# Scatters of the second-order records moved from the adjacency stage to the propagation layers, through HBM in chunks of 50 columns

## The chip, the cores and the metric

The kernel runs on one core of one Trainium2 chip, as one program. The metric is the time of one execution in microseconds (us); smaller is better. The engines are TensorE (PE, with its weight loads as PEld), VectorE (DVE), ScalarE (ACT), GpSimd (POOL) and SyncE (SP). SP and ACT issue plain DMAs, POOL issues indirect ones (a row of an HBM table per partition, by an index) and, after the change, plain ones too. All of them run on the core's 16 DMA engines.

## The reference, cut to what matters

The input is a graph of 3125 nodes with 48 features each and 100,000 edges (`src`, `dst`, 40 attributes, a type of 8, two weights). Four graph layers follow one another, and after each the result is added to `x` and normalized:

1. an attention network with a gate on each edge and four rounds of attention;
2. a propagation with K = 5 steps, each a sum over the edges with weights from the degrees;
3. a propagation with K = 10 steps, weighted by `edge_weight`;
4. a relation layer.

The last one is what the moved scatters are for:

```python
h1 = relu(einsum('ni,rij->nrj', x, weight1) + bias1)
h2 = einsum('nrj,rjo->nro', h1, weight2)
msg = h2[src, rel_type] * edge_weight1
agg = segment_sum(msg, dst, num_segments=3125)
x = layernorm(x + relu(agg + bias2))
```

## The kernel before, in words

Nodes are cut into 25 blocks of 128 (`NB`). The edges lie in SBUF as 125 partitions by 800 columns (`EP`, `ET`): column t holds 125 edges. Two orders of the edges are made and written to HBM as tables of records:

- `REC`, the first order: a record of 104 numbers for each edge, sorted by pair of source and destination block, in 1488 tiles of 128 edges, four tiles to a group (372 groups).
- `REC2`, the second order: a record of 4 numbers for each edge (weight, two lanes, an index), sorted by destination block, in 816 tiles (204 groups). Only the relation pass reads it, at the very end.

The stages follow one another. Each is a function with a block of its own, and all engines meet at a block's end.

- **`sort_edges`** works out the places. It fills `meta` (6 numbers an edge, 125 x 800 x 6) and at its end `place2` (one index an edge), both kept in SBUF until `adjacency` is done. Its second block runs 25 laps of 4 slots; in each slot POOL waits for semaphores of three kinds of work and then issues 8 scatters into `REC` (L455), one for each column, 800 in all.
- **`tile_tables`** makes small tables.
- **`adjacency`** runs over the 372 groups of the first order. ACT loads a group's records (L763), VectorE builds one-hot matrices (L820, L826, L832), PE transposes them (L791, L792) and multiplies them (L800, L801), ACT copies the transposes (L775) and stores them to `OHT` (L777), VectorE adds the products into `acc` (L846, four to a group), and SP stores each of the four sums to `ADJ` (L737). The order of work on each engine is written out by hand (`in_turns`), with four slots. Beside it, POOL runs a loop of its own: it issues 800 scatters of the second order (L746), one for each column, without a wait between them, and then waits for all of them (L750). Nothing else in the stage needs their result.
- The attention stages follow. From `start_nodes` on, `mem["sums"]` holds 25 x 49 numbers in each partition; attention writes and reads it, the propagation layers don't touch it, and the relation pass writes it again at its end.
- **`propagate`** (L1798) is called twice, with 5 steps and one round for the degrees, and with 10 steps: 16 rounds in all. In a round PE multiplies the features of each of the 25 source blocks with that block's row of the dense `ADJ` (L1874; a row is 1600 KB). Seven of the rows stay in SBUF (`held`, loaded by ACT, L1901). The other 18 pass through three slots: SP waits until PE has used a slot (`s_used`) and loads the next row (L1845). At the end of a round VectorE combines the sums (L1966 and its like), PE transposes them back (L1893), and ACT copies them to the features for the next round (L1908). POOL has nothing to do in it.
- **`relation_nodes`** computes `h2` and stores it.
- **`relation_pass`** runs over the 204 groups of `REC2`: SP loads the records (L2092), POOL gathers four times 128 rows of `h2` (L2104), VectorE makes one-hots and messages (L2135, L2138), and PE adds them up (L1228).

Of the kernel before, what the change touches and what calls it, by code (L numbers as in the profile page):

```python
# [17 lines left out]
I32 = mybir.dt.int32  # L18
# [14 lines left out]
EP = 125  # L33
ET = E // EP
# [8 lines left out]
CW, W, NORM, SL, DL, GIDX = 50, 51, 52, 53, 54, 55  # L43
GATES = 56
RW = GATES + H
META = GATES - CW
# [7 lines left out]
FIRST = 2048  # L54
SW = H + 1
SPB = 10
ROW = 2 * P * NB
HOT = 3
CAP = 60.0
# [648 lines left out]
def adjacency(nc, mem):  # L708
# [3 lines left out]
    with ExitStack() as ctx:  # L712
        room = Room(nc, ctx, "a_")
# [6 lines left out]
        ptr = [room.ps(f"ptr{b}", [P, G, 2, P], BF16) for b in range(2)]  # L720
        sums = [room.ps(f"sums{b}", [P, G, 2 * P]) for b in range(2)]
        s_rec, s_oht, s_out = ([room.sem(f"{name}{b}") for b in range(SLOTS)] for name in ("s_rec", "s_oht", "s_out"))
        s_second = [room.sem(f"s_second{b}") for b in range(4)]
        s_hs, s_wide, s_hot, s_ptr, s_sums, s_turned, s_acc, s_init = (
            room.sem(n) for n in ("s_hs", "s_wide", "s_hot", "s_ptr", "s_sums", "s_turned", "s_acc", "s_init"))

# [14 lines left out]
        with nc.Block() as block:  # L741
            @block.gpsimd
            def _(pool):

                for t in range(ET):
                    nc.gpsimd.indirect_dma_start(  # L746
                        out=mem["REC2"], out_offset=bass.IndirectOffsetOnAxis(ap=mem["place2"][:, t:t + 1], axis=0),
                        in_=mem["meta"][:, t, NORM - CW:META], in_offset=None).then_inc(s_second[t % 4], 16)
                for b in range(4):
                    pool.wait_ge(s_second[b], 16 * ET // 4)  # L750

            @block.sync
            def _(sp):
# [103 lines left out]
def scratch(nc):  # L857

    def dram(name, shape, dt=F32):
        return nc.dram_tensor(name, shape, dt, kind="Internal").ap()  # L860

    mem = {}
    mem["REC"] = dram("REC", [T * P, RW])
    mem["REC_G"] = mem["REC"].rearrange("(g p r) w -> g p (r w)", p=P, r=G)
    mem["REC2"] = dram("REC2", [T2 * P, META - 2])
    mem["REC2_G"] = mem["REC2"].rearrange("(g p r) w -> g p (r w)", p=P, r=G)
    mem["OHT"] = dram("OHT", [NG, P, G * HOT * P], BF16)
    mem["H2"] = dram("H2", [NB * P, RELS * H])
    mem["ADJ"] = dram("ADJ", [(NB + 2) * ROW, P])
    for name, shape, dt in (("ident_bf", [P, P], BF16), ("ident_hf", [P, P], F16), ("ident", [P, P], F32),  # L870
                            ("apart", [P, P], BF16), ("upper", [P, P], F32), ("lower", [P, P], F32),
                            ("iota", [P, P], F32), ("iota_bf", [P, P], BF16), ("cap", [P, G], F32)):
        mem[name] = nc.alloc_sbuf_tensor("m_" + name, shape, dt)
    return mem
# [93 lines left out]
def nodes(ap):  # L968

    return ap.rearrange("p c w -> p (c w)")  # L970
# [824 lines left out]
                norm(nc, dve, ch, sc, out, mem["x"][:])  # L1795


def propagate(nc, mem, half, steps, degrees):  # L1798


    SLOTS = 3
# [9 lines left out]
    with ExitStack() as ctx:  # L1811
# [6 lines left out]
        if degrees:  # L1818
# [4 lines left out]
        s_used, s_f, s_dve, s_deg, s_root, s_x, s_up, s_back, s_sum = (  # L1823
            room.sem(n) for n in ("s_used", "s_f", "s_dve", "s_deg", "s_root", "s_x", "s_up", "s_back", "s_sum"))
        s_tick = room.sem("s_tick")
        acc = room.ps("acc", [P, FOURS, 512])
        back = room.ps("back", [P, 2, 2, 512])
        rows = mem["ADJ"][0:NB * ROW].rearrange("(s p h d) c -> s p h (d c)", s=NB, p=P, h=2)
# [10 lines left out]
        with nc.Block() as block:  # L1839
            @block.sync  # L1840
            def _(sp):
                with sp.Fori(0, rounds) as k:
                    for m, s in enumerate(PASSING):
                        sp.wait_ge(s_used, k * len(PASSING) + m + 1)
                        sp.dma_start(row[:, m % SLOTS], rows[s, :, half]).then_inc(s_row[m % SLOTS], 16)  # L1845

            @block.tensor
            def _(pe):
# [332 lines left out]
def gnn_stack(nc, io, out):  # L2181
    mem = scratch(nc)
# [14 lines left out]
            attention_pass(nc, mem, layer)  # L2197
            update(nc, mem, io, layer)
    residual_norm(nc, mem, mem["x"][:], mem["h"][:], 0)
    propagate(nc, mem, 0, 5, 1)  # L2200
    residual_norm(nc, mem, mem["x"][:], mem["h"][:], 1)
    propagate(nc, mem, 1, 10, 0)
    residual_norm(nc, mem, mem["x"][:], mem["h"][:], 2)
    relation_nodes(nc, mem, io)
    relation_pass(nc, mem)
# [26 lines left out]
```

## Time and profile before

| what | value |
|---|---|
| time of 3 runs, median (lowest to highest) | 11525.92 us (11525.92 to 11526.84) |
| time of the profiled execution | 11507.11 us |
| span of the profiled execution | 11505.3 us |
| PE, DVE, ACT, POOL busy, share of the span | 70%, 55%, 29%, 40% |
| adjacency stage, with POOL's scatters | 1595 to 2787 us |
| adjacency stage, after them | 2790 to 3936 us |
| first and second propagation layer | 8680 to 9242 us, 9259 to 10062 us |

The profile comes from one execution. Its span is the time from the first instruction to the last that the trace shows, and the program's own time is 1.8 us longer. A row of a view groups instructions: the line of the kernel, the engine, the operation, the tile written and those read, the count; then the busy time and the mean duration of one; then the idle time of the engine just before them and what ended it. `issue` means that the engine waited for nothing that the profile shows, `remote` that a semaphore was set from elsewhere. Tile names carry the prefix of their stage: `a_` adjacency, `p_` propagation, `l_` relation pass. The tables `REC` and `REC2` have one name in the rows, `REC`. Stages are told apart by their windows, in us from the start of the span.

### The profile page before, as it was taken

What the parts mean: (1) busy time and instruction counts of PE and PEld (TensorE: products, weight loads), DVE (VectorE), ACT (ScalarE), POOL (GpSimd) and SP (SyncE); (2) the same over time, 40 slices, a digit from 0 to 9 for tenths busy, and PEclk for the clock granted to TensorE, in tenths of its full rate; (3) what the DMA queues carried; (4) which work ended last, traced back from release to release, by engine and by line L of the source; (5) the groups of instructions that cost most, each with busy time, mean ns of one, the idle gap of its engine ahead of it and who ended that gap; (6) DMA issues with size and microseconds to landing.
All of it is one profiled execution on the core that took longest, in us unless ns stands there. A gap on an engine that the chain in (4) does not pass through costs nothing. (4 is left out here: it accounts for less than half of the span.)

```text
span 11505.3 us, 328287 instructions
## 1 busy us (share of the span) xinstructions
PE 8060.2 (70%) x107650; PEld 6419.3 (56%) x107651; DVE 6381.7 (55%) x21371; ACT 3299.7 (29%) x11512; POOL 4649.4 (40%) x6184
## 2 busy tenths in 40 slices
PE   2999943234777588499599769949967889962323
PEld 1777732223555477499489659938963444443323
DVE  6444453335999767688678958868872010011112
ACT  3222211112333233266256536626640000010000
POOL 0777767775000166255145415514530000026665
PEclk9999985555767699799699879969988999955555
DMA  7222223334777699399279649928957889801112
GB/s 293 59 59 59 59 59 79 72 81 120 222 223 222 179 292 311 101 248 248 71 215 248 177 111 248 248 60 226 247 141 294 356 343 372 354 24 18 18 18 18
DMA packets 2228522, 1954.48 MB, mean 170 GB/s; under 512 B 1472897, under 2 KB 1871505, under 8 KB 2189698
## 3 DMA queue, kind: packets, MB, share of 16 engines
q1 hardware_dynamic: 1872642, 1712.86, 48.6%
q10 hardware_dynamic: 252000, 173.83, 4.9%
q0 software_dynamic: 103712, 65.58, 3.8%
q8 instruction: 102, 1.67, 0.1%
q14 instruction: 66, 0.54, 0.0%
HBM read 1478.99 MB, written 470.93 MB: 169 GB/s over the span
## 5 line engine op out<-in xcount | busy, mean ns | idle before, releaser
L1615 POOL TENSOR_TENSOR s_rest<-s_msg 128x196 f32<-128x196 f32 x1488 | 764.3, 514 | 2232.9 <-ACT s_msg L1597 1821.5
L2104 POOL DMA_INDIRECT l_row<-H,l_rec x816 | 786.9, 964 | 2158.9 <-DMA l_rec<-REC 1839.1
L1214 PE MATMUL s_gotd<-m_table_d,s_hot 128*128 x17856 | 1423.5, 205 | 201.1 <-DMA s_hot<-OHT 193.4
L1597 ACT ACTIVATE s_msg<-s_gotd,s_es 128x49 f32<-128x49 f32 x5952 | 1310.0, 304 | 48.7 <-ACT s_es L1590 0.5
L1214 PE MATMUL s_small<-m_table_s,s_hot 128*128 x17856 | 1301.6, 185 | 0.7 <-issue 0.2
L1214 PEld LDWEIGHTS s_gotd<-m_table_d,s_hot 128*128 128x128 bf16 x17856 | 1030.8, 96 | 399.0 <-issue 233.4
L846 DVE SCALAR_TENSOR_TENSOR a_acc<-a_acc,m_keep,a_sums 128x256 f32<-128x256 f32 x1488 | 707.2, 475 | 807.8 <-remote 751.6
L455 POOL DMA_INDIRECT REC<-rec,place x800 | 949.8, 1187 | 322.7 <-issue 215.1
L746 POOL DMA_INDIRECT REC<-m_meta,m_place x800 | 951.0, 1189 | 294.9 <-issue 243.6
L791 PE MATMUL a_ptr<-m_ident_bf,a_hd 128*128 128x128 bf16 x1488 | 295.0, 275 | 1094.3 <-DVE a_hd_weighted L832 756.0
L1648 DVE TENSOR_REDUCE s_tops<-s_mt 128x512 f32 (+1 forms) x1488 | 1014.7, 682 | 2.0 <-PE s_mt L1558 1.7
L1214 PEld LDWEIGHTS s_small<-m_table_s,s_hot 128*128 128x128 bf16 x17856 | 1002.9, 97 | 13.8 <-issue 1.7
L1228 PE MATMUL l_sums<-l_msg,l_oh 128*128 128x49 f32 x1632 | 372.1, 382 | 833.3 <-issue 792.0
L1874 PE MATMUL p_acc<-p_row,p_feats 128*64 128x512 f32 (+1 forms) x4032 | 883.0, 565 | 102.5 <-DMA p_row<-ADJ 101.0
L801 PE MATMUL a_sums<-a_hd_weighted,a_hs_wide 128*128 128x128 f32 x2976 | 864.2, 421 | 48.6 <-issue 47.8
L791 PEld LDWEIGHTS a_ptr<-m_ident_bf,a_hd 128*128 128x128 bf16 x1488 | 176.3, 123 | 1203.2 <-DVE a_hd_weighted L832 606.5
L1228 PEld LDWEIGHTS l_sums<-l_msg,l_oh 128*128 128x128 f32 x1632 | 376.2, 323 | 830.5 <-issue 830.4
L1558 PE MATMUL s_mt<-m_ident_bf,s_raw 128*128 128x128 bf16 x5952 | 826.3, 219 | 0.9 <-issue 0.9
L1557 PE MATMUL s_mt<-s_hot,m_apart 128*128 128x128 bf16 x5952 | 824.5, 219 | 1.3 <-issue 0.7
L1622 POOL TENSOR_TENSOR s_least<-s_rest 128x196 bf16<-128x196 f32 x1488 | 765.0, 514 | 116.8
L801 PEld LDWEIGHTS a_sums<-a_hd_weighted,a_hs_wide 128*128 128x128 f32 x2976 | 702.4, 288 | 107.5 <-issue 56.9
L1874 PEld LDWEIGHTS p_acc<-p_row,p_feats 128*64 128x64 f32 x4032 | 392.3, 140 | 574.7 <-issue 394.3
(414 smaller groups left out, 19900.6 us busy)
## 6 DMA issues: line engine op xcount, KB each, us to landing
s_hot<-OHT SPq DMA_DIRECT2D x1488, 384.0 KB
p_row<-ADJ SPq DMA_DIRECT2D x288, 1600.0 KB
ADJ<-a_acc SPq DMA_DIRECT2D x1488, 128.0 KB
s_rec<-REC SPq DMA_DIRECT2D x1488, 98.0 KB
OHT<-a_turned ACTq DMA_DIRECT2D x372, 384.0 KB
g_hot<-OHT SPq DMA_DIRECT2D x372, 384.0 KB
REC<-fill SPq DMA_DIRECT2D x124, 624.0 KB, 10.2
g_rec<-REC SPq DMA_DIRECT2D x372, 108.0 KB
```

What stands on the lines that cost most here:

```text
L455: nc.gpsimd.indirect_dma_start(out=mem["REC"], out_offset=bass.IndirectOffsetOnAxis(ap=place[:, b, j:j + 1], axis=0), in_=rec[:, b, j], in ...
L746: nc.gpsimd.indirect_dma_start(out=mem["REC2"], out_offset=bass.IndirectOffsetOnAxis(ap=mem["place2"][:, t:t + 1], axis=0), in_=mem["meta" ...
L801: last = nc.tensor.matmul(sums[b % 2][:, j, P:2 * P], hs_wide[:, b % 2, j], hd_weighted[:, b % 2, j], start=True, stop=True)
L1214: last = nc.tensor.matmul(out, hot, table[k][:, bass.ds(at, w)], start=(k == 0), stop=(k == 2))
L1557: nc.tensor.matmul(mt[:, j], mem["apart"][:], hot[:, b, j, 1], start=True, stop=False)
L1558: last = nc.tensor.matmul(mt[:, j], upper(raw[:, b % KEPT, j:j + 1]).to_broadcast([P, P]), mem["ident_bf"][:], start=False, stop=True)
L1597: last = nc.scalar.activation(msg[:, b % KEPT, j], gotd[b % KEPT][:, j, SW:2 * SW], ACT.Copy, scale=es[:, b % 2, j:j + 1])
L1615: nc.gpsimd.tensor_tensor(rest[:, b % KEPT].rearrange("p g w -> p (g w)"), msg[:, b % KEPT].rearrange("p g w -> p (g w)"), upper(msg[:, b ...
L1622: nc.gpsimd.tensor_tensor(least[:, b % KEPT].rearrange("p g w -> p (g w)"), rest[:, b % KEPT].rearrange("p g w -> p (g w)"), upper(rest[:, ...
L1648: v.tensor_reduce(tops[:, bass.ds(n, 1)], mt[:].rearrange("p j e -> p (j e)"), X, ALU.max).then_inc(s_top, 1)
L1874: last = nc.tensor.matmul(acc[odd * SIDE:(odd + 1) * SIDE, q, 0:n * P].rearrange("w (c e) -> w c e", e=P), feats[:, s], source.rearrange(" ...
L2104: nc.gpsimd.indirect_dma_start(out=row[:, b, j], out_offset=None, in_=table, in_offset=bass.IndirectOffsetOnAxis(ap=rec[:, b, j, GIDX - NO ...
```

## The change

The scatters leave `adjacency`. In their place POOL writes `meta` and `place2` to two new HBM tensors and waits for both. `propagate` takes a further argument, a range of chunks of 50 columns: 6 chunks (300 scatters) for the first call, 10 chunks (500 scatters) for the second. In its block POOL loads a chunk's numbers and places into one of two halves of `mem["sums"]` and issues the chunk's 50 scatters; the loads of the next chunk are issued ahead of them, after a wait until the scatters of the chunk before, which used the same half, have landed. At the end POOL waits for all scatters. No other engine gets or loses an instruction.

```diff
--- before.py
+++ after.py
@@ -54,6 +54,7 @@
 FIRST = 2048
 SW = H + 1
 SPB = 10
+CHUNK = 50
 ROW = 2 * P * NB
 HOT = 3
 CAP = 60.0
@@ -720,7 +721,7 @@
         ptr = [room.ps(f"ptr{b}", [P, G, 2, P], BF16) for b in range(2)]
         sums = [room.ps(f"sums{b}", [P, G, 2 * P]) for b in range(2)]
         s_rec, s_oht, s_out = ([room.sem(f"{name}{b}") for b in range(SLOTS)] for name in ("s_rec", "s_oht", "s_out"))
-        s_second = [room.sem(f"s_second{b}") for b in range(4)]
+        s_second = room.sem("s_second")
         s_hs, s_wide, s_hot, s_ptr, s_sums, s_turned, s_acc, s_init = (
             room.sem(n) for n in ("s_hs", "s_wide", "s_hot", "s_ptr", "s_sums", "s_turned", "s_acc", "s_init"))
 
@@ -742,12 +743,9 @@
             @block.gpsimd
             def _(pool):
 
-                for t in range(ET):
-                    nc.gpsimd.indirect_dma_start(
-                        out=mem["REC2"], out_offset=bass.IndirectOffsetOnAxis(ap=mem["place2"][:, t:t + 1], axis=0),
-                        in_=mem["meta"][:, t, NORM - CW:META], in_offset=None).then_inc(s_second[t % 4], 16)
-                for b in range(4):
-                    pool.wait_ge(s_second[b], 16 * ET // 4)
+                nc.gpsimd.dma_start(mem["META"], mem["meta"][:]).then_inc(s_second, 16)
+                nc.gpsimd.dma_start(mem["PLACE2"], mem["place2"][:]).then_inc(s_second, 16)
+                pool.wait_ge(s_second, 32)
 
             @block.sync
             def _(sp):
@@ -864,6 +862,8 @@
     mem["REC_G"] = mem["REC"].rearrange("(g p r) w -> g p (r w)", p=P, r=G)
     mem["REC2"] = dram("REC2", [T2 * P, META - 2])
     mem["REC2_G"] = mem["REC2"].rearrange("(g p r) w -> g p (r w)", p=P, r=G)
+    mem["META"] = dram("META", [EP, ET, META])
+    mem["PLACE2"] = dram("PLACE2", [EP, ET], I32)
     mem["OHT"] = dram("OHT", [NG, P, G * HOT * P], BF16)
     mem["H2"] = dram("H2", [NB * P, RELS * H])
     mem["ADJ"] = dram("ADJ", [(NB + 2) * ROW, P])
@@ -1795,7 +1795,7 @@
                 norm(nc, dve, ch, sc, out, mem["x"][:])
 
 
-def propagate(nc, mem, half, steps, degrees):
+def propagate(nc, mem, half, steps, degrees, chunks):
 
 
     SLOTS = 3
@@ -1823,6 +1823,12 @@
         s_used, s_f, s_dve, s_deg, s_root, s_x, s_up, s_back, s_sum = (
             room.sem(n) for n in ("s_used", "s_f", "s_dve", "s_deg", "s_root", "s_x", "s_up", "s_back", "s_sum"))
         s_tick = room.sem("s_tick")
+        s_chunk = [room.sem(f"s_chunk{b}") for b in range(2)]
+        s_second = [room.sem(f"s_second{b}") for b in range(2)]
+        moved = nodes(mem["sums"][0:EP])
+        numbers_of = [moved[:, b * CHUNK * META:(b + 1) * CHUNK * META].rearrange("p (t w) -> p t w", w=META)
+                      for b in range(2)]
+        places_of = [moved[:, (2 * META + b) * CHUNK:(2 * META + b + 1) * CHUNK].bitcast(I32) for b in range(2)]
         acc = room.ps("acc", [P, FOURS, 512])
         back = room.ps("back", [P, 2, 2, 512])
         rows = mem["ADJ"][0:NB * ROW].rearrange("(s p h d) c -> s p h (d c)", s=NB, p=P, h=2)
@@ -1843,6 +1849,30 @@
                     for m, s in enumerate(PASSING):
                         sp.wait_ge(s_used, k * len(PASSING) + m + 1)
                         sp.dma_start(row[:, m % SLOTS], rows[s, :, half]).then_inc(s_row[m % SLOTS], 16)
+
+            @block.gpsimd
+            def _(pool):
+
+                def fetch(n):
+                    b, cols = n % 2, slice(chunks[n] * CHUNK, (chunks[n] + 1) * CHUNK)
+                    if n >= 2:
+                        pool.wait_ge(s_second[b], 16 * CHUNK * (n // 2))
+                    nc.gpsimd.dma_start(numbers_of[b], mem["META"][:, cols]).then_inc(s_chunk[b], 16)
+                    nc.gpsimd.dma_start(places_of[b], mem["PLACE2"][:, cols]).then_inc(s_chunk[b], 16)
+
+                fetch(0)
+                for n in range(len(chunks)):
+                    b = n % 2
+                    if n + 1 < len(chunks):
+                        fetch(n + 1)
+                    pool.wait_ge(s_chunk[b], 32 * (n // 2) + 32)
+                    pool.sem_inc(s_tick, 1)
+                    for t in range(CHUNK):
+                        nc.gpsimd.indirect_dma_start(
+                            out=mem["REC2"], out_offset=bass.IndirectOffsetOnAxis(ap=places_of[b][:, t:t + 1], axis=0),
+                            in_=numbers_of[b][:, t, NORM - CW:META], in_offset=None).then_inc(s_second[b], 16)
+                for b in range(2):
+                    pool.wait_ge(s_second[b], 16 * CHUNK * len(chunks[b::2]))
 
             @block.tensor
             def _(pe):
@@ -2197,9 +2227,9 @@
             attention_pass(nc, mem, layer)
             update(nc, mem, io, layer)
     residual_norm(nc, mem, mem["x"][:], mem["h"][:], 0)
-    propagate(nc, mem, 0, 5, 1)
+    propagate(nc, mem, 0, 5, 1, range(0, 6))
     residual_norm(nc, mem, mem["x"][:], mem["h"][:], 1)
-    propagate(nc, mem, 1, 10, 0)
+    propagate(nc, mem, 1, 10, 0, range(6, ET // CHUNK))
     residual_norm(nc, mem, mem["x"][:], mem["h"][:], 2)
     relation_nodes(nc, mem, io)
     relation_pass(nc, mem)
```

## Rows read from the trace of the kernel before

**Rows 1.** The page's head: span, busy time and share of each engine.
```profile
span 11505.3 us, 328287 instructions
...
PE 8060.2 (70%) x107650; PEld 6419.3 (56%) x107651; DVE 6381.7 (55%) x21371; ACT 3299.7 (29%) x11512; POOL 4649.4 (40%) x6184
```

**Rows 2.** Windows: sort, adjacency (two parts), propagation (two layers), relation.
```profile
core 0: us, PE busy (x) PEld busy (x) DVE busy (x) ACT busy (x) POOL busy (x), PEclk, DMA share, GB/s
260.00:1590.00 1330.00, 1252.78 (x5200) 916.18 (x5200) 648.37 (x3133) 276.34 (x401) 954.23 (x803) 1.00 0.24 56
1595.00:2787.00 1192.00, 379.08 (x1990) 300.82 (x1991) 418.24 (x1593) 160.84 (x198) 948.75 (x799) 0.53 0.36 78
2790.00:3936.00 1146.00, 829.51 (x5440) 674.03 (x5440) 1091.08 (x4354) 417.35 (x545) 0.00 (x0) 0.70 0.75 222
8680.00:9242.00 562.00, 458.18 (x2259) 223.94 (x2257) 65.78 (x93) 11.65 (x27) 0.00 (x0) 0.92 0.81 331
9259.00:10062.00 803.00, 740.19 (x3750) 362.86 (x3746) 20.76 (x40) 14.15 (x41) 0.00 (x0) 0.98 0.92 373
10272.00:11482.00 1210.00, 375.67 (x1637) 377.24 (x1635) 204.56 (x410) 0.00 (x0) 786.86 (x816) 0.50 0.13 18
```

**Rows 3.** Groups by line, adjacency: two rows of 1595 to 2787, one after.
```profile
L746 POOL DMA_INDIRECT REC<-m_meta,m_place x799 | 949.8, 1189 | 243.6 <-issue 243.6
...
L846 DVE SCALAR_TENSOR_TENSOR a_acc<-a_acc,m_keep,a_sums 128x256 f32<-128x256 f32 x392 | 186.9, 477 | 768.8 <-remote 749.9 <-issue 4.2 <-PE a_sums L801 3.3
...
L846 DVE SCALAR_TENSOR_TENSOR a_acc<-a_acc,m_keep,a_sums 128x256 f32<-128x256 f32 x1095 | 519.8, 475 | 37.2 <-PE a_sums L801 0.6
```

**Rows 4.** Waits of 1595 to 2787: us in total, times, longest.
```profile
DVE a_acc L846 <- remote: 749.9, 94, 12.5
ACT a_hs_wide L769 <- remote: 518.6, 94, 10.2
...
POOL REC L746 <- issue: 243.6, 799, 0.3
```

**Rows 5.** DMA queues of 1595 to 2787 (SP's, ACT's, POOL's).
```profile
q1 hardware_dynamic: 106080, 51.14, 14.7%
q10 hardware_dynamic: 67296, 39.79, 11.5%
q0 software_dynamic: 25536, 2.52, 9.3%
```

**Rows 6.** Window in the first propagation layer, row loads back to back.
```profile
8692.00:8776.00 84.00, 68.02 (x310) 30.82 (x308) 0.00 (x0) 0.00 (x0) 0.00 (x0) 0.94 0.99 407
```

**Rows 7.** Waits of the relation pass, 10272 to 11482.
```profile
DVE l_oh L2135 <- DMA REC<-m_meta,m_place: 541.8, 39, 21.4
DVE l_msg L2138 <- DMA l_row<-H,l_rec: 264.2, 72, 6.2
```

**Rows 8.** The page's DMA issues: KB each, us to landing.
```profile
REC<-fill SPq DMA_DIRECT2D x124, 624.0 KB, 10.2
```

**Rows 9.** Waits of both propagation layers, 8670 to 10070.
```profile
PE p_acc L1874 <- DMA p_row<-ADJ: 101.0, 101, 10.6
```

**Rows 10.** Groups by line of the sort stage, 260 to 1590.
```profile
L455 POOL DMA_INDIRECT REC<-rec,place x800 | 949.8, 1187 | 322.7 <-issue 215.1 <-DVE rec L559 107.6
```

**Rows 11.** Groups by line of the relation pass.
```profile
L2104 POOL DMA_INDIRECT l_row<-H,l_rec x816 | 786.9, 964 | 2158.9 <-DMA l_rec<-REC 1839.1 <-issue 254.0 <-DVEq L2140 65.7
L1228 PEld LDWEIGHTS l_sums<-l_msg,l_oh 128*128 128x128 f32 x1632 | 376.2, 323 | 830.5 <-issue 830.4
```

## The prediction, made before the change was run

> **What bounds the kernel now.** I read the page's busy shares first: no engine is busy over 70% of the span, so the kernel is a row of stages with different limits [rows 1], and each has to be read alone. The windows by stage come next [rows 2]: in the first part of the adjacency stage (1595 to 2787) VectorE is busy 418 us of 1192, in the second (2790 to 3936) 1091 of 1146. The reader is to see that POOL is busy only in the first, and that both parts do the same work. The groups by line give the pace: 392 of the 1488 updates of `acc` (L846, four to a group) fall into the first part, 1095 into the second [rows 3]. That is 98 groups at 1192 / 98 = 12.16 us, and 274 at 1146 / 274 = 4.18 us. The waits say who holds the slow part up: not the scatters' data (nobody waits for it there), but `remote`, 749.9 us in 94 waits, 8 us each [rows 4]. Transfers are not short of engines either: the DMA engines are busy 0.36 of it, of which the scatters' queue takes 9.3% [rows 2, 5]. So POOL's 800 scatters, one each 1.189 + 0.305 = 1.49 us [rows 3, 4], slow the other engines 2.9 times without using up anything that the profile shows as full.
>
> **Removed.** 800 scatters leave the adjacency stage. The 98 groups then run at the pace of the other 274, VectorE's: 98 x 4.18 = 410 us instead of 1192, so **782 us less**. This holds if nothing else slows a group; the second part shows that for 1146 us on end.
>
> **Added in the adjacency stage.** Two POOL DMAs, `meta` (125 x 19,200 bytes) and `place2` (125 x 3,200), 2.8 MB together. At the 407 GB/s of a full stretch [rows 6] that is 7 us of the DMA engines, which the stage otherwise uses to 0.75 [rows 2]. VectorE covers it; without cover it costs 7. I take 3. POOL's wait for both has nothing behind it until the block ends, 1500 us later.
>
> **Added in the propagation layers.** POOL has no work there now (x0 in both rows) [rows 2]. It gets 6 chunks in the first and 10 in the second, each of two loads (150 KB and 25 KB) and 50 scatters.
> - *POOL's own time.* First layer: 300 x 1.49 = 448 us in a stage of 562. Second: 500 x 1.49 = 747 us in one of 803. To this comes, per chunk, the issue of two loads and the wait until the scatters of the chunk before have landed; what is queued behind that wait is the next chunk's own scatters, no other engine. No POOL load of this kind is in the trace: the issue lies between 0 and two scatters (2.4 us); landings lie between the 3.7 us for which VectorE waited on a gather on average (264.2 / 72) and the 10.2 us of a far larger fill [rows 7, 8]. With 2.4 + 3.7 the ten chunks come to 61 us, POOL to 808 us; with 10.2, to 873. I take the nearer row, the gather: POOL ends with the layer and costs 0 to 5 us (70 at the far end). The load of chunk n + 1 has the 75 us of chunk n to land.
> - *DMA engines.* A second-layer round takes 80.3 us, and in it they are busy 0.92 [rows 2]; with 9.3% for the scatters [rows 5], 1.013. PE is also at 740 of 803 us, and of its waits on row loads there are 101 us in the two layers together [rows 9]. The least cost is the excess, 1.3% of 1192 us = 15. The most by this route is that all of the share is added to each round: 9.3% of 1192 = 111 us. The first layer has some room (0.81), the second none, so I take **85 us**, in the upper half.
> - *SP and ACT.* The scatters are on no queue of theirs. The 18 passing rows of a round go through SP, with three slots.
>
> **Sum.** Against the profiled execution's 11507.1 us (span 11505.3 and 1.8 around it): - 782 + 3 + 85 + 2 = 10,815. The median of the runs lies 18.8 above that execution, so the forecast is 10,834, **10,835 us**. Its own range, with 0 to 7, 15 to 111 and 0 to 70 as ends, is 10,760 to 10,930.
>
> **Where the choice lies.** The sum takes it that the scatters' harm stays behind. The trace has three stages with POOL DMAs back to back, and they disagree. *For:* in the sort stage POOL issues 800 scatters of the same duration, 1.187 us, beside a PE that is busy 1253 of 1330 us with 3.9 matmuls a microsecond at a granted clock of 1.00 (2.4 GHz) [rows 2, 10]. The second propagation layer asks 4.7 [rows 2], much the same load. POOL there waits for others just 107.6 us [rows 10]. *Against:* the adjacency stage, above, and the relation pass, where 816 gathers at 0.964 us run beside a PE that stands 830 us with no releaser shown, and VectorE waits 541.8 us in 39 waits of 14 us each (the row puts them down to scatters long done); PE's clock is 0.50 (1.2 GHz) [rows 2, 7, 11]. In the sort stage POOL must pause each 8 scatters for its waits; in the change it runs 50 without one. A propagation layer has few handovers, though: 18 row loads and one turn of the round in 80 us, where an adjacency group issues six DMAs in 12.
>
> The Trainium skill ("SBUF — State Buffer", Who interferes with whom) has one rule, that only the port pair of VectorE and GpSimd causes contention and that PE and ACT wait on nobody. Taken alone it gives the sum above. The trace does not bear it out: in the adjacency stage PE does 1.67 matmuls a microsecond while POOL issues, and 4.75 after [rows 2].
>
> **Rival 1, handovers late, still faster.** A slot is reused each 80.3 / 18 x 3 = 13.4 us. Its chain is a transfer (1600 KB at 407 GB/s, 4.0 us), PE's use (740 / 250 = 3.0) and two handovers; I allow 2 us for these as they are. An adjacency group pays 12.16 - 4.18 = 8 us over some three handovers in series, so about 3 us each, an estimate. Then the slot takes 9 + 6 = 15 us, 12% over, and the turn of a round (PE, DVE, PE, ACT, PE) 4 x 3 = 12 more: 90 + 12 = 102 us, a factor of 1.27. In 1192 us of scatters that loses 1192 x (1 - 1/1.27) = 253 us: 11507 - 782 + 253 + 5 + 19 = **11,000**. For it: rows 4. Against: the sort stage.
> The Trainium skill ("DMA: Bandwidth & Descriptors", Queues, rings and completion order) names a way: a semaphore increment is a strongly ordered write that lands after all earlier writes of that DMA engine, over its queues. A row load's landing would then wait for scatter writes to HBM. That is this rival, at the same price; no row shows single landings.
>
> **Rival 2, starved, slower.** PE in the propagation layers does no better beside POOL than in the relation pass: 1637 matmuls in 1210 us, 1.35 a microsecond against 4.67 [rows 2]. Over 1192 us that is 1613 matmuls, the work of 345 us, and loses 847. A clock at 0.50 would go with it. Time: 11507 - 782 + 847 + 5 + 19 = **11,596**, and up to 11,940 if rounds stand still for all 1192 us. It decides from a factor of 2.9, where 1192 x (1 - 1/2.9) = 781 eats the whole gain: which is the adjacency stage's own factor, so this lies near. For it: both stages without pauses for POOL suffer. Against: few handovers, and PE's dense work in the sort stage.
>
> **Rival 3, no change**: the factor is just the adjacency stage's, 2.84 by matmuls (4.75 / 1.67): loss 772, time 11,521.
>
> **Rival 4, the gain isn't there**: the first part is slow for another reason. Then the time is 11,526 + 85. The pace changes within the microseconds in which POOL ends [rows 2, 3], so 1 in 50; it counts as slower.
>
> **Numbers.** Forecast case 0.44; rival 1 (spread 10,930 to 11,480) 0.29; rival 3 0.05; rival 2 0.20; rival 4 0.02. About 0.2%, 23 us, is what a measurement of this kernel tells from no change. Faster 0.73, same 0.05, slower 0.22. The range reaches from 10,745, a little under the forecast's own, to 11,560, which leaves out most of rival 2, somewhat under 2 in 10.
>
> **What would show it.** Right: the adjacency stage takes some 1560 us with VectorE over 0.9 busy throughout; a second-layer round takes 82 to 89 us; PE's granted clock stays at 0.95 or over; POOL's scatters still take 1.19 us and end before the layer. Rival 1: rounds of 95 to 130 us while POOL issues, 80 after, with SP or PE waiting for handovers. Rival 2: rounds over 230 us, PE's clock near 0.5, and a quick tail after POOL's last scatter. POOL as the bound: the layer ends just behind its last landing. The forecast is wrong as a whole if the 98 groups don't come down to about 4.2 us.

## The result, and the profile after it

The median goes from 11,526.4 us (4 runs, 11,525.9 to 11,538.6) to **10,817.5 us** (4 runs, 10,811.3 to 10,821.5): a ratio of 0.938, 95% interval 0.937 to 0.940. The forecast was 10,835 us. On one of the chips of the later runs the same pair came out the other way round, the changed kernel 0.5% slower; that is the main finding below.

Of the changed kernel first the page's head, then the windows of the same four stages (columns as in [rows 2]):

```profile
span 10809.5 us, 328339 instructions
PE 7991.0 (74%) x107650; PEld 6355.4 (59%) x107651; DVE 6360.2 (59%) x21371; ACT 3284.0 (30%) x11512; POOL 4657.1 (43%) x6218
```
```profile
1595.00:3100.00 1505.00, 1080.60 (x7145) 879.31 (x7146) 1428.96 (x5719) 546.78 (x715) 0.00 (x0) 0.71 0.75 222
7914.00:8491.00 577.00, 467.57 (x2268) 223.40 (x2266) 56.22 (x81) 9.67 (x24) 364.87 (x308) 0.92 0.87 327
8517.00:9368.00 851.00, 742.97 (x3731) 355.80 (x3732) 20.38 (x39) 13.48 (x36) 597.77 (x515) 0.98 0.95 360
9580.00:10786.00 1206.00, 372.74 (x1637) 378.37 (x1635) 204.49 (x410) 0.00 (x0) 786.81 (x816) 0.50 0.13 18
```

The adjacency stage has no slow first part any more: VectorE is busy 1429 of 1505 us throughout. POOL's work is now in the two propagation layers, whose DMA share rose from 0.81 and 0.92 [rows 2] to 0.87 and 0.95. PE's granted clock stays at 0.92 and 0.98. The relation pass is as before.

Four more views. Three are of the second layer (8517 to 9368): a group by line, the DMA queues, a row of POOL's waits. The last is a row of PE's waits in both layers (7900 to 9380):

```profile
L1871 POOL DMA_INDIRECT REC<-m_sums x499 | 588.7, 1180 | 213.0 <-issue 213.0
```
```profile
q1 hardware_dynamic: 25896, 294.62, 89.6%
q0 software_dynamic: 16614, 2.98, 3.4%
q10 hardware_dynamic: 763, 8.54, 2.4%
```
```profile
POOL m_sums L1860 <- DMA REC<-m_sums: 40.2, 8, 5.7
```
```profile
PE p_acc L1904 <- DMA p_row<-ADJ: 160.3, 110, 11.9
```

A scatter still takes POOL 1.18 us, but 213.0 / 499 = 0.43 us pass between two of them instead of 0.30 [rows 4]; its eight waits until a chunk's scatters have landed are 5 us each. POOL's queue, scatters and chunk loads together, takes 3.4% of the DMA engines, not 9.3% [rows 5]. PE's waits on row loads grew from 101.0 us [rows 9] to 160.3.

### The profile page after: what moved, and what is told of

Its sections match the earlier page's. It is cut to its first block and busy times, and to the rows that moved or that the text cites. A ratio compares the mean times of both kernels' runs of the same rounds, so it can differ in the third digit from the quotient of the medians.

```text
span 10809.5 us, 328339 instructions
## 1 busy us (share of the span) xinstructions
PE 7991.0 (74%) x107650; PEld 6355.4 (59%) x107651; DVE 6360.2 (59%) x21371; ACT 3284.0 (30%) x11512; POOL 4657.1 (43%) x6218
## 5 line engine op out<-in xcount | busy, mean ns | idle before, releaser
L1871 POOL DMA_INDIRECT REC<-m_sums x800 | 950.1, 1188 | 355.2 <-issue 348.1
L1904 PE MATMUL p_acc<-p_row,p_feats 128*64 128x512 f32 (+1 forms) x4032 | 898.9, 569 | 162.5 <-DMA p_row<-ADJ 160.3
L1228 PE MATMUL l_sums<-l_msg,l_oh 128*128 128x49 f32 x1632 | 369.0, 378 | 832.4 <-issue 809.0
L1228 PEld LDWEIGHTS l_sums<-l_msg,l_oh 128*128 128x128 f32 x1632 | 377.4, 322 | 825.4 <-issue 825.4
L799 PE MATMUL a_sums<-a_hd_weighted,a_hs_wide 128*128 128x128 f32 x2976 | 802.6, 403 | 0.0
L799 PEld LDWEIGHTS a_sums<-a_hd_weighted,a_hs_wide 128*128 128x128 f32 x2976 | 661.4, 274 | 45.9
L1578 PE MATMUL s_sums<-s_msg,s_hot 128*128 128x49 bf16 x5952 | 619.6, 186 | 63.3 <-issue 48.2
```

The source lines that it names most:

```text
L799: last = nc.tensor.matmul(sums[b % 2][:, j, P:2 * P], hs_wide[:, b % 2, j], hd_weighted[:, b % 2, j], start=True, stop=True)
L1871: nc.gpsimd.indirect_dma_start(out=mem["REC2"], out_offset=bass.IndirectOffsetOnAxis(ap=places_of[b][:, t:t + 1], axis=0), in_=numbers_of[ ...
L1904: last = nc.tensor.matmul(acc[odd * SIDE:(odd + 1) * SIDE, q, 0:n * P].rearrange("w (c e) -> w c e", e=P), feats[:, s], source.rearrange(" ...
```

## The stages of all kernels

Each stage from its first busy instruction to the end of its block, waits at that end included, in us, from the profiled execution. Six kernels have a single run in place of a median: pause each 8, fixed store places, split 3 and 13, 16 rows, POOL copies and plain DMAs. Chip 1 and chip 2 are the chips of the first and second set of runs, chip 3 that of the third; the first pair was measured apart from them, on a chip that is called the first one here.

| kernel | chip | adjacency | layer 1 | layer 2 | relation | median |
|---|---|---|---|---|---|---|
| before | first | 2344.9 | 556.3 | 821.4 | 1213.0 | 11,526 |
| after | first | 1576.3 | 585.1 | 865.8 | 1209.0 | 10,818 |
| after, no scatters | 1 | 1576.4 | 564.7 | 838.2 | 1361.2 | 10,911 |
| before, no scatters | 1 | 1566.5 | 552.6 | 827.4 | 1363.3 | 10,883 |
| before, pause each 8 | 1 | 1955.4 | 557.1 | 830.5 | 1217.4 | 11,138 |
| before, fixed store places | 1 | 2317 (+ 200 zeroing) | 552.0 | 822.7 | 1205.9 | 11,670 |
| before, paced | 2 | 1619.7 | 553.5 | 825.1 | 1218.4 | 10,788 |
| after, split 7 and 9 | 2 | 1576.8 | 610.8 | 865.6 | 1209.8 | 10,844 |
| after, split 3 and 13 | 2 | 1576.8 | 571.7 | 1102.2 | 1207.9 | 11,035 |
| before, 16 rows | 2 | 2607.5 | 557.2 | 825.5 | 1331.0 | 11,894 |
| before, POOL copies | 3 | 2200.5 | 560.7 | 819.9 | 1363.4 | 11,521 |
| before, plain DMAs | 3 | 1745.5 | 555.7 | 818.9 | 1065.8 | 10,759 |
| after, again | 3 | 1576.9 | 583.8 | 869.5 | 1059.9 | 10,661 |
| before, paced, again | 3 | 1599.2 | 555.9 | 821.8 | 1061.9 | 10,612 |

The kernel before, run beside each set, took 11,536.4 us on chip 1, 11,543.8 on chip 2 and **10,612.4 on chip 3**. In the two kernels that ran on two chips the relation pass takes some 150 us less on chip 3; the adjacency stage of the kernel before took some 745 less there, as is worked out below. All stages but these two agree within 0.5%.

## Experiments on chip 1: is it the scatters, and what about them?

**After, no scatters.** The 50 `indirect_dma_start` of each chunk left out, the chunk loads and the two stores kept.

> The changed kernel with its 800 scatters left out (the second order's records keep their fill values); the stores of META and PLACE2 and the chunk loads stay. Theory A: what the two propagation layers lost (28.9 and 44.5 us, together 73.4) is the scatters' own doing, by their share of the DMA engines. Then the layers come back to 556 and 822 us, rounds of 84.2 and 78.4 us, and the time is 10,817.5 - 73 = 10,745 (10,735 to 10,760). Theory B: part of the loss is from the chunk loads of 125 partitions or from the layer's longer program. Then less than 50 us come back and the time is above 10,770.

**Before, no scatters.** The `@block.gpsimd` of the adjacency stage emptied.

> The kernel before with its 800 scatters and POOL's waits for them left out (the second order's records keep their fill values). Theory A: the scatters alone made the adjacency stage slow. Then its pace is 4.2 us a group from first to last, the stage comes to 1,565 us from 2,341, and the time is 11,526 - 770 - 4 = 10,752 (10,735 to 10,765), about the same as the run without scatters in the layers. Theory B: something else in the stage (the address loads, the small stores) takes part. Then the stage keeps more than 1,650 us and the time is above 10,840.

Both times miss, by a side effect: the relation pass takes 1361 and 1363 us instead of 1209 to 1217. Where REC2 keeps its fill, each gather reads the same row; that this is why was not tried. So the stages decide. Without scatters the adjacency stage takes 1566.5 us, as theory A has it. The layers without scatters take 1402.9 us together, against 1450.9 with them and 1374.7 to 1387.6 in the five kernels that have no POOL work there on chips 1 and 2, 1380.7 on average. So the loss is **48 us for the scatters and 22 for the chunk loads**, from one trace of each kernel; the five differ by 13 us among themselves, so both can be off by some 7. By its own line, under 50 us coming back, the expectation's theory B came out: the chunk loads have a part in it, a third.

Two small terms show in the waits. First the adjacency stage's first 55 us, changed kernel, then the one without scatters or stores; below, the wait of the layer's opening, with and without chunk loads (both without scatters):

```profile
DVE a_turned L818 <- DMA a_rec<-REC: 12.7, 2, 10.7
```
```profile
DVE a_turned L815 <- DMA a_rec<-REC: 2.0, 1, 2.0
```
```profile
DVE p_factor L1973 <- PE p_acc L1898: 105.7, 1, 105.7
```
```profile
DVE p_factor L1944 <- PE p_acc L1869: 97.5, 1, 97.5
```

The stores of META and PLACE2 go ahead of the first record loads and hold VectorE for 10.7 us: this is about the whole difference of 1576.4 to 1566.5. The first chunk's loads put the first rows of a layer back by 8 us; the second layer's opening lost 10.7 likewise (102.4 to 113.1 us). The scatters lengthen every round instead: in the second layer from 79 us to 82.1 (before: 78.4).

**Before, pause each 8.**

```diff
                 for t in range(ET):
+                    if t >= 8 and t % 8 == 0:
+                        for b in range(4):
+                            pool.wait_ge(s_second[b], 16 * t // 4)
```

> The kernel before, but POOL waits after every 8 scatters until all have landed. Theory A (pauses): the harm in the adjacency stage comes from scatters issued without a pause, so that the other engines' handovers pile up behind them; with pauses a group takes 4.2 to 5 us beside the scatters, POOL ends at 100 x (8 x 1.49 + 3 to 6) = 1,500 to 1,800 us, and the stage at 1,600 to 1,850: time 10,780 to 11,040. Theory B (a price for each scatter): 800 scatters cost the others 0.97 us each wherever they stand, the stage keeps about 2,340 us and the time is 11,480 to 11,560. Between: 11,200 would be half and half.

**Before, fixed store places.** `at = [NB * ROW + b * G + j for j in tiles]` in place of the values loaded from `entry`, and a block ahead of it that fills ADJ with zeros.

> The kernel before, but the ADJ stores go to fixed spare places (so SP loads no addresses from SBUF), and ADJ is filled with zeros ahead of the stage, 82 MB in 50 stores, 200 to 260 us (ADJ so holds zeros where the sums of pairs belong). Theory A (address loads): SP's loads of register values are what falls behind beside the scatters; without them a group takes 4.2 to 5 us beside the scatters, the stage 1,570 to 1,650 us, the time 11,526 - 730 + 230 = about 11,030. Theory B (handovers of all engines, or the DMA engines): they make no difference, 12 us a group beside the scatters, stage about 2,340 us, time about 11,755.

To compare, VectorE's updates of `acc` in the same 800 us (1800 to 2600; 2000 to 2800 with the zeroing) by the groups of lines. Before, with pauses, with fixed places, changed:

```profile
L846 DVE SCALAR_TENSOR_TENSOR a_acc<-a_acc,m_keep,a_sums 128x256 f32<-128x256 f32 x259 | 123.6, 477 | 522.9 <-remote 511.0 <-issue 4.1
```
```profile
L849 DVE SCALAR_TENSOR_TENSOR a_acc<-a_acc,m_keep,a_sums 128x256 f32<-128x256 f32 x558 | 265.4, 476 | 207.2 <-remote 87.9 <-DMA ADJ<-a_acc 62.7 <-PE a_sums L804 21.0
```
```profile
L858 DVE SCALAR_TENSOR_TENSOR a_acc<-a_acc,m_keep,a_sums 128x256 f32<-128x256 f32 x273 | 129.8, 476 | 511.7 <-remote 499.4 <-PE a_sums L813 3.2
```
```profile
L844 DVE SCALAR_TENSOR_TENSOR a_acc<-a_acc,m_keep,a_sums 128x256 f32<-128x256 f32 x765 | 363.3, 475 | 25.4
```

The address loads are not it: 273 updates against 259. Pauses are half of it: 558, and `remote` falls from 511 to 88 us. The stage took 1955 us, between the theories of 1,600 to 1,850 and 2,340. The same 800 scatters cost 389 us instead of 778, 0.49 us each: there is no fixed price for a scatter; it depends on how they follow each other.

What `remote` hides can be read from the semaphores. All 94 of VectorE's `remote` waits in the slow part [rows 4] end with an update of one semaphore, the one that TensorE sets behind its last product of a group (L801), and that update comes 5.0 us on average after the recorded end of its instruction. So `remote` is nothing from elsewhere here, but TensorE, recorded too late to be matched. The 39 long waits of the relation pass [rows 7] end with an update of TensorE's (L1228) as well. Four lines of the kernel before, one group, show it:

```profile
2213.05 0.37 PE L801 MATMUL a_sums<-a_hd_weighted,a_hs_wide 128*128 128x128 f32 x1 [1.05 <-issue]
2219.69 0.62 ACT L769 CAST a_hs_wide<-a_turned 128x512 f32<-128x512 bf16 x1 [6.31 <-remote]
2219.83 0.48 DVE L846 SCALAR_TENSOR_TENSOR a_acc<-a_acc,m_keep,a_sums 128x256 f32<-128x256 f32 x1 [9.88 <-remote]
2222.56 0.29 PE L791 MATMUL a_ptr<-m_ident_bf,a_hd 128*128 128x128 bf16 x1 [9.13 <-issue]
```

TensorE's last product ends at 2213.4, its update is recorded at 2219.6, and ACT and VectorE go on at once. The way back is prompt: VectorE ends the group's last one-hot at 2222.50 and TensorE starts at 2222.56; over 48 groups this takes 0.08 us on average, as in the fast part. The lateness for 1800 to 2400 (fixed places 2000 to 2600), from the end of the last instruction that sets the semaphore to the recorded update, with how many updates were recorded of those that the instructions made (the kernels on chips 2 and 3 are explained further down):

| kernel | chip | TensorE's updates: recorded, us late | VectorE's: recorded, us late |
|---|---|---|---|
| before | first | 88 of 95, 4.5 | 105 of 286, 0.01 |
| before, fixed store places | 1 | 98 of 101, 3.9 | 146 of 305, 0.01 |
| before, pause each 8 | 1 | 184 of 210, 2.1 | 278 of 630, 0.01 |
| before, 16 rows | 2 | 21 of 21, 25.2 | 19 of 60, 0.01 |
| before, paced | 2 | 173 of 278, 0.43 | 411 of 834, 0.01 |
| before, paced, again | 3 | 257 of 281, 0.01 | 818 of 841, 0.01 |
| after | first | 287 of 287, 0.01 | 859 of 859, 0.01 |

In the kernel before, the transposes' update (L792) is 3.7 us late on average and the products' (L801) 5.3, together about the 12.2 - 4.2 = 8 us that a group loses. The ends of matmuls are modelled, so the trace can't tell a TensorE that finishes late from a signal that is held back. And where the stage is slow, update records are missing as well. That the recording itself has a part in the harm is a rival that no run here tests.

## Experiments on chip 2: density, and POOL's place in the layers

**Before, paced.**

```diff
                 for t in range(ET):
+                    if t > 0:
+                        pool.wait_ge(s_acc, 9 * t // 5)
```

> The kernel before, but each scatter of the adjacency stage waits until VectorE has added up 9 tiles for every 5 scatters, so that the 800 are spread evenly over the stage, one in 1.9 us instead of one in 1.49 us. Theory A (backlog): what harms is a POOL that issues without a gap; evenly spread, the handovers keep up, a group takes 4.2 to 4.6 us, the stage 1,570 to 1,720 us, and the time is 10,750 to 10,900: with a stage below 1,640 us it beats the changed kernel. Theory B (a price for each scatter, of which the pauses of 4 us after 8 scatters took away only half, 0.97 to 0.49 us): the spread ones cost 0.3 to 0.5 us each, the stage 1,800 to 1,970 us, time 10,990 to 11,150. Theory C (a full price): stage 2,340 us, 11,526.

**Before, 16 rows.** `place2[0:16, t:t + 1]` and `meta[0:16, t, ...]` in the scatter; the other rows are left out.

> The kernel before with scatters of 16 rows instead of 125 (the other 109 rows of each column aren't written and keep their fill values): the same 800 instructions on POOL, an eighth of the packets. Theory A (what counts is how POOL and its queue are kept busy, instruction by instruction): POOL still takes about 1.2 + 0.3 us each, the stage still loses 600 to 780 us. Theory B (what counts is the packets, their writing and their landing): the loss falls with the rows to about 100 us: stage 1,600 to 1,700 us. POOL's own time for one is read beside it: if it falls well below 1.19 us the two theories share what is left, and the loss over POOL's total busy time is to be compared (before: 778 us over 800 x 1.19 = 951 us).

The same 800 us, paced and then with 16 rows, and of the latter POOL's row as well:

```profile
L848 DVE SCALAR_TENSOR_TENSOR a_acc<-a_acc,m_keep,a_sums 128x256 f32<-128x256 f32 x742 | 352.2, 475 | 29.7 <-remote 3.5 <-issue 2.5 <-DVE a_acc L848 1.2
```
```profile
L746 POOL DMA_INDIRECT REC<-m_meta,m_place x566 | 602.3, 1064 | 197.7 <-issue 197.7
...
L846 DVE SCALAR_TENSOR_TENSOR a_acc<-a_acc,m_keep,a_sums 128x256 f32<-128x256 f32 x56 | 26.7, 478 | 733.9 <-remote 732.2
```

Spread over the stage, the scatters cost 53 us (1619.7 against 1566.5 with none, on chip 1): theory A. **This kernel does the whole work, without the way by HBM, and is faster than both**: 10,788.5 us (10,779.9 to 10,798.1), 0.935 of the kernel before measured beside it, interval 0.933 to 0.936. With 16 rows the loss grew instead of falling to an eighth: a scatter in 800 / 566 = 1.41 us instead of 1.49, and 56 updates instead of 259. The stage took 2607.5 us, more than either theory gave. This refutes a price by packets or bytes, and with the paced and the paused one it makes a row: one scatter in 1.41, 1.49, 800 / 453 = 1.77 (on average) and 1.94 us; 56, 259, 558 and 742 updates. That density alone makes this row isn't shown: the first of the four differs in its rows too, the third in its pauses.

**After, split 7 and 9, and 3 and 13.** Only the ranges in `gnn_stack` change: `range(0, 7)` and `range(7, ...)`; `range(0, 3)` and `range(3, ...)`.

> The changed kernel with 7 chunks in the first propagation layer and 9 in the second, instead of 6 and 10. If POOL is inside both layers (350 x 1.49 us + 12 us = 534 us of about 588, 450 of about 862) and each scatter costs the layers the same, about 0.06 us beside PE, the time stays at 10,817 (10,808 to 10,825). If POOL's end set the second layer's end (its last scatter went out in the layer's last 5 us), a few us come back: 10,800 to 10,812.

> The changed kernel with 3 chunks in the first propagation layer and 13 in the second, so that 650 scatters stand in a layer of 866 us. If POOL keeps the pace that it had beside that layer (500 scatters in 851 us, 1.70 us each), it needs 1,105 + 8 us, the layer about 1,118 us, the first layer 570: time 10,817 + 252 - 15 = 11,054. If POOL was held up only by PE's stream and goes at 1.49 us, it needs 650 x 1.49 + 20 = 990 us: time 10,926. If POOL's place doesn't matter (no bound by its own time), the time is about 10,817.

First and last scatter of a layer (duration min/median/max, first and last start) for 7 and 9 in the first layer, then windows of its end and of the second layer's end for 3 and 13:

```profile
L1871 POOL DMA_INDIRECT REC<-m_sums x350: 1172/1178/2885, 7920.0 to 8517.5; - x175
```
```profile
8490.00:8516.00 26.00, 2.30 (x25) 2.04 (x25) 4.39 (x10) 2.65 (x5) 19.02 (x16) 0.50 0.08 2
```
```profile
9250.00:9350.00 100.00, 90.23 (x457) 42.70 (x458) 2.08 (x4) 1.54 (x4) 69.29 (x60) 1.00 0.92 342
9365.00:9590.00 225.00, 0.00 (x0) 0.00 (x0) 0.00 (x0) 0.00 (x0) 173.00 (x148) 0.50 0.09 3
```

Both show POOL as the bound. From the first of its 350 scatters to the last POOL needs 597.5 us, 1.71 each, and the layer waits for it, 610.8 instead of 585.1 us: my 534 us, at 1.49 a scatter, was wrong. With 650 it runs on for some 240 us behind PE's last matmul; 11,035 us is the 1.70 us reading (11,054), not the 1.49 one (10,926). And 50 scatters fewer in the second layer gave nothing back (865.6 to 865.8; the 3 us that they should be worth beside PE are less than the 9 us by which this layer differs between like kernels). So POOL's end had not set that layer's end in the changed kernel, and its trace shows how near it was: POOL was through at 9370.3, ACT's last copy at 9371.0. In the first layer POOL issued its last scatter at 8431.2, 62 us before the end. With 6 and 10 chunks POOL has room in the first layer and just fits into the second.

## Experiments on chip 3: where the harm isn't

**Before, POOL copies.** The scatter replaced by

```diff
+                    nc.gpsimd.tensor_copy(idle[:, t % 4], mem["meta"][:, 0:200].rearrange("p t w -> p (t w)")
+                                          ).then_inc(s_second[t % 4], 1)
```

> The kernel before with 800 copies of 125 x 1200 numbers on POOL in place of its 800 scatters (the second order's records keep their fill values, which makes the relation pass some 150 us longer, as in the two runs without scatters). POOL is as busy as before, but issues no DMA. Theory A (the scatters' issue): no handover falls behind, VectorE's operations may get longer where both engines read at once, the stage takes 1,570 to 1,700 us, time 10,885 to 11,020. Theory B (a busy POOL is enough, by a port or a bus that it shares): the stage takes over 2,000 us, time over 11,300.

**Before, plain DMAs.**

```diff
+                    nc.gpsimd.dma_start(mem["REC2"][t * EP:(t + 1) * EP], mem["meta"][:, t, NORM - CW:META]
+                                        ).then_inc(s_second[t % 4], 16)
```

> The kernel before with plain DMAs issued by POOL in place of the scatters: column t goes to rows 125 t to 125 t + 124 of REC2 (so the second order isn't sorted), the same rows and bytes, without an index. Such an issue took POOL 0.6 us for META and PLACE2, so 800 of them go out in 500 to 1,200 us. Theory A (POOL's software DMAs without a gap, whatever their kind): the stage is as slow beside them as beside the scatters, 10 to 14 us a group or more, and loses 400 to 900 us: stage 1,970 to 2,470, time 11,150 to 11,650. Theory B (only the indirect form, its index read and address work): a group takes 4.2 to 5 us, stage 1,570 to 1,680, time 10,745 to 10,860.

**After, again**, and **before, paced, again**, unchanged.

> The changed kernel once more, beside the paced one on the same chip: 10,817 (10,805 to 10,830).

> The kernel before with its scatters paced by VectorE's progress (9 tiles for 5 scatters), once more, beside the changed kernel on the same chip. Its stage lost 53 us where the changed kernel loses 10 us in that stage and 71 in the layers, so it is 28 us ahead: 10,788 (10,778 to 10,800). If the lead was the chips' difference, both are within 8 us of each other.

The kernel before takes 10,612.4 us here (15 runs, 10,603.8 to 10,620.6), 0.92 of its time elsewhere. Against it the **change is slower**, by a small step that is clear of noise: 10,660.7 us, ratio 1.0048, interval 1.0034 to 1.0062. The paced one is the same as before: 10,612.0 us, 1.0002, 0.9993 to 1.0011. The expectations of the last two miss in level, by 156 and 176 us; that the paced one leads the changed one holds, by 49 us instead of 28.

The layers and the adjacency stage of the changed kernel are what they were. What differs is the relation pass, which takes 1060 us instead of 1209 in the same code, and the adjacency stage of the kernels that have their scatters there. The sort stage, with 800 scatters in bursts of 8, takes 1532 us on both. Waits of that pass, changed kernel, on the first chip (9600 to 10700) and on chip 3 (9600 to 10600):

```profile
DVE l_oh L2165 <- remote: 578.4, 51, 21.5
...
DVE l_msg L2168 <- DMA l_row<-H,l_rec: 176.8, 60, 4.0
```
```profile
DVE l_msg L2168 <- DMA l_row<-H,l_rec: 732.0, 195, 4.3
```

On chip 3 VectorE waits 195 times, 3.8 us each, for what it needs, the gather. On the first chip 51 waits of 11 us come before that, and all of them end with an update by TensorE (L1228 there, the products of the messages), which comes 13.5 us on average after the recorded end of its last instruction; on chip 3 all 196 of TensorE's updates come within 0.1 us. ACT's waits in the paced kernel's adjacency stage (1700 to 2300), chip 2 and then chip 3:

```profile
ACT a_hs_wide L771 <- issue: 225.6, 82, 3.3
...
ACT a_hs_wide L771 <- DVE a_turned L822: 133.1, 50, 3.3
```
```profile
ACT a_hs_wide L771 <- DVE a_turned L822: 359.3, 130, 3.2
...
ACT a_hs_wide L771 <- issue: 26.0, 10, 2.9
```

These are about the same in all, 377 and 385 us with the small rows; `issue` stands where no update was recorded that could have ended the wait. So they show no lateness of VectorE, only that records are missing on chip 2. TensorE's updates differ: 0.43 us late on average on chip 2, 0.01 on chip 3. **So the harm shows as late completions of TensorE, and chip 3 doesn't have them.** Since the paced kernel and the one before agree there, and differ in nothing but the pacing, the stage must have taken about 1,600 us in the one before too; this is worked out from times, as no trace of it was taken on that chip. Whether the chip itself differs, or something that ran on it or beside it, stays open, and so does what makes TensorE's completions late.

The other two ran where there were no late completions, so they say nothing on those, and theory A and B of both stay undecided for the slow chips: the copies' 2200.5 us lie in theory B's range, but by another cause, and the plain DMAs' 1745.5 in neither's. They show two other prices. First a VectorE group beside POOL's copies (1700 to 2300), the same group beside paced scatters on chip 3, and in the changed kernel without either (both 1800 to 2600):

```profile
L822 DVE TENSOR_SCALAR a_turned<-m_iota_bf,a_rec 128x128 bf16<-128x128 bf16 x172 | 163.0, 1011 | 2.1 <-issue 2.1
...
L848 DVE SCALAR_TENSOR_TENSOR a_acc<-a_acc,m_keep,a_sums 128x256 f32<-128x256 f32 x174 | 82.1, 472 | 5.8
```
```profile
L822 DVE TENSOR_SCALAR a_turned<-m_iota_bf,a_rec 128x128 bf16<-128x128 bf16 x748 | 163.3, 338 | 9.7 <-issue 9.7
```
```profile
L818 DVE TENSOR_SCALAR a_turned<-m_iota_bf,a_rec 128x128 bf16<-128x128 bf16 x764 | 140.7, 248 | 10.1 <-issue 10.1
```

Beside copies of 1.18 us VectorE's operation on SBUF takes 1011 ns instead of 248, the one that reads PSUM 472, as ever: the stage came to 2200 us, and every recorded update of VectorE, ACT and TensorE was prompt, 0.01 us. Scatters cost a little of the same, 338 ns; that this is most of the 33 us by which the paced stage stays above 1566.5 on chip 3 isn't shown. Here the Trainium skill ("SBUF — State Buffer", Who interferes with whom) fits the trace: an exclusive lock on the port pair that VectorE and GpSimd share, held for a whole instruction. The trace shows the times, not the lock.

Plain DMAs cost 179 us (1745.5 against 1566.5). DMA queues of 1700 to 2300:

```profile
q1 hardware_dynamic: 119014, 57.38, 57.3%
q10 hardware_dynamic: 72592, 43.77, 37.3%
q0 software_dynamic: 20032, 1.30, 4.7%
```

The two queues of the loads and stores hold the engines 94.6% for 101 MB; in the changed kernel, in the same window, it was 74.7% for 133 MB. There the DMA engines became the bound, beside 617 issues of 533 ns each on POOL.

## Why the prediction was right, point by point

- **The sum.** That 10,835 came so near to 10,817.5 us is in part luck, since errors cancelled: the adjacency stage gave back 10 us less than forecast, the layers cost 14 us less (73 instead of 85 + 2), the relation pass came out 4 us shorter, and the median lies 6 us above the profiled execution instead of 19.
- **Removed, 782 us less.** Right on the first chip: VectorE's first operation of the next stage starts at 3169.8 instead of 3938.3, 768.5 us earlier; with the 10 us below that is 778. The bound was named rightly too, VectorE at 0.95. But the step was taken for a property of the kernel. It is one of the kernel on a chip: on chip 3 the same step is worth 22 us (1599.2, paced, to 1576.9).
- **Adjacency, + 3 for the stores.** Wrong in size, 10 us: "VectorE covers it" fails in the stage's first microseconds, when nothing is in flight and the first record load queues behind 2.8 MB.
- **DMA engines, + 85.** 73.2 us came (1377.7 to 1450.9), well inside 15 to 111, but not by its working. The 9.3% was the share beside a stage of small transfers; beside the row loads it is 3.4%. Added to the rounds in full, which is the upper reading, 3.4% of 1428 us is 48.6, and 48 was measured; that is one agreement, found afterwards, and no run tests the rule. The missing term is the chunk loads' 22 us, mostly at the openings, which the step didn't price at all. And its round of 80.3 us held the layer's opening; between two turns it was 78.4.
- **POOL's own end, 0 to 5 us.** The cost was right, the pace wrong: 1.71 us a scatter, not 1.49. Its last scatter goes out at 9366.5 in a layer that ends at 9371.4. One chunk more in the first layer bounds that layer, three more the second. The far end, 70 us, was nearer than it was made to look.
- **Rival 1, handovers late.** Its rounds of 102 us did not come (82.1 in the second layer, 87.9 in the first), nor did **rivals 2 and 3**. The argument used, that a layer has few handovers, isn't what the traces bear out: the completions themselves were not late there. On the first chip 160 updates of TensorE on the rows of the second layer are recorded (of 179), 0.03 us late on average and 0.9 at most, where the adjacency stage had 4.5. Why they are prompt beside scatters of 1.71 us each isn't shown. The price of rival 1 had the right size, though, for the stage it was taken from: the 8 us of a slow group are not some three handovers of 3 us each but mainly two of TensorE's, late by 3.7 and 5.3 us. The rule of the Trainium skill ("DMA: Bandwidth & Descriptors", Queues, rings and completion order) that was named beside rival 1 stays open: PE's waits on rows grew by 59 us, far from the rival's 253, and no view shows what part of them is a landing held up by the scatters' writes.
- **Slower, 0.22.** The case that did come about on chip 3, + 48 us, was none of the rivals: the costs of the change in the layers with almost none of its main gain. Rival 4 had that form (11,526 + 85), with 1 in 50, for the reason that the pace changes as POOL ends. That is sound for one chip, and nothing in one chip's profile could tell of another.

## What to carry to other kernels

Where other engines stand in `remote` waits while POOL issues indirect DMAs back to back, ask first which semaphore ends the waits, and how long after its engine's last instruction. Then spread the DMAs before you move them: one wait a scatter, on the progress of the engine that sets the pace, took back 725 of 778 us where the harm was (stages from three chips) and cost nothing measurable where it wasn't. Before a large gain by such a move is believed, time the pair on a second chip. A share of the DMA engines doesn't carry over from one stage to another: the queue of the same scatters took 9.3% beside small transfers and 3.4% beside row loads.

## What was not expected of the hardware

- The two kernels that ran on two chips each: the sort stage, the attention stages taken together (4739 and 4743 us in the changed kernel) and the propagation layers are equal within 0.5%. Others with indirect DMAs are not: adjacency differs by 1.3% paced, the relation pass by 14%, and the adjacency stage of the kernel before by some 745 us of 2345, worked out as above.
- On the first chip, beside back-to-back scatters, an update by TensorE comes 4.5 us on average after the recorded end of its instruction, while those by VectorE and ACT that are recorded come within 0.02 us.
- On a chip with late completions, scatters of 16 rows do more harm than scatters of 125: 56 updates in 800 us are 14 groups at 57 us each, against 259 updates, 12.4 us.
- POOL's scatters come further apart beside full row loads (0.43 us between two instead of 0.30), with 1.18 us each in both.
